# Cross-attention on one core: shared products issued whole at the end of a head, value bias on TensorE, residual and row normalisation off VectorE

## What is computed

```python
q = jnp.einsum('oc,bct->bot', Wq, target) + bq[None, :, None]
k = jnp.einsum('oc,bcs->bos', Wk, source) + bk[None, :, None]
v = jnp.einsum('oc,bcs->bos', Wv, source) + bv[None, :, None]
...
dot = jnp.einsum('bhdt,bhds->bhts', q, k) / math.sqrt(HEAD_DIM)
mask = target_mask[:, :, :, None] * source_mask[:, :, None, :]
dot = mask * dot - (1.0 - mask) * NEG
amap = jax.nn.softmax(dot, axis=-1) * mask
out = jnp.einsum('bhts,bhds->bhdt', amap, v)
```

## Time and profile before

| what | value |
|---|---|
| median of 3 runs | 3245.24 us (3241.58 to 3249.78) |
| profiled execution | 3250.03 us, span 3248.2 us |
| TensorE busy | 2971.8 us, 91% |
| VectorE busy | 2824.2 us, 87% |
| ScalarE busy | 2360.5 us, 73% |
| GpSimd busy | 1990.9 us, 61% |
| attention stage | about 1757 to 2836 us of the span |

### The profile page before, as it was taken

One profiled execution on the slowest core, in us unless ns is written; L12 is line 12 of the kernel. 1 busy time (PEld: TensorE's weight loads), 2 busy tenths in 40 slices (PEclk: granted clock), 3 DMA queues, 4 the chain that ended last, 5 costly groups with the idle time before them and its releaser, 6 DMA issues. The chain is left out here.

```text
span 3248.2 us, 47812 instructions
## 1 busy us (share of the span) xinstructions
PE 2971.8 (91%) x16101; PEld 1814.1 (56%) x16134; DVE 2824.2 (87%) x4149; ACT 2360.5 (73%) x4499; POOL 1990.9 (61%) x1071
## 2 busy tenths in 40 slices
PE   8899999999999999999976998888889888789998
PEld 5677777776777767776653433333333333244444
DVE  6999999999999999999995788888788888188886
ACT  5888888888888888888871366666666666567876
POOL 4999999999999999999993132232223222100000
PEclk9999999999999999999986699999999999899999
DMA  4202220122202220122224455555555553131111
GB/s 172 68 9 78 82 79 28 61 79 79 73 18 78 82 79 32 58 79 79 86 78 115 126 164 168 179 173 161 173 163 169 167 179 92 65 109 46 43 43 36
DMA packets 138148, 312.49 MB, mean 96 GB/s; under 512 B 20240, under 2 KB 27536, under 8 KB 137760
## 3 DMA queue, kind: packets, MB, share of 16 engines
q1 hardware_dynamic: 132544, 300.05, 29.3%
q10 hardware_dynamic: 5360, 9.38, 1.0%
HBM read 217.42 MB, written 91.95 MB: 95 GB/s over the span
## 5 line engine op out<-in xcount | busy, mean ns | idle before, releaser
L823 POOL TENSOR_TENSOR bu<-du,bc 128x1024 f32<-128x1024 f32 x512 | 1199.4, 2372 | 32.3 <-DMA bc<-bc_scratch 32.0
L710 ACT ACTIVATE states<-dt,negA 128x256 f32<-128x256 f32 x2048 | 852.6, 463 | 239.5 <-DVE hc L918 229.0
L1560 DVE TENSOR_REDUCE mmax<-s_ps 128x1 f32<-128x512 f32 x1024 | 671.7, 685 | 202.8 <-PE s_ps L1292 185.5
L906 DVE TENSOR_TENSOR_SCAN states<-states,bu 128x512 f32<-128x512 f32 x704 | 821.4, 1212 | 9.0 <-ACT states L710 8.1
L1416 ACT ACTIVATE pt<-s_ps 128x512 f32<-128x512 f32 x1024 | 549.0, 595 | 342.6 <-PE s_ps L1302 341.7
L918 DVE TENSOR_TENSOR hc<-states,bc 128x512 f32<-128x512 f32 x704 | 445.2, 673 | 1.2 <-DMA bc<-bc_scratch 1.2
L1292 PE MATMUL s_ps<-kst,qst 51*128 51x512 f32 x1024 | 400.0, 470 | 40.8 <-DMA kst<-mask_d 21.4
L528 PEld LDWEIGHTS y_ps<-id_sb,hc 128*128 128x128 f32 x2816 | 331.1, 143 | 122.4 <-DVE hc L918 58.0
L528 PE MATMUL y_ps<-id_sb,hc 128*128 128x128 f32 x2816 | 377.1, 277 | 23.4 <-DVE hc L918 23.4
L1302 PE MATMUL s_ps<-qst,kst 53*128 53x512 f32 x1024 | 385.5, 455 | 4.3 <-ACT pt L1416 4.3
L832 POOL TENSOR_TENSOR hp<-hp,bc 128x1024 f32<-128x1024 f32 x160 | 379.7, 2373 | 1.6 <-DVE hp L906 1.1
(11 more groups left out here) (164 smaller groups left out, 4218.8 us busy)
## 6 DMA issues: line engine op xcount, KB each, us to landing
bc<-bc_scratch SPq DMA_DIRECT2D x128, 512.0 KB, 5.0
stack_d<-parts SPq DMA_DIRECT2D x90, 512.0 KB, 3.8
qst<-stack_d SPq DMA_DIRECT2D x128, 192.0 KB
kst<-stack_d SPq DMA_DIRECT2D x128, 192.0 KB
x<-xres SPq DMA_DIRECT2D x31, 512.0 KB, 4.4
w_raw<-in_w_ffn SPq DMA_DIRECT2D x48, 256.0 KB, 2.7
w_raw<-in_w_ffn SPq DMA_DIRECT2D x16, 768.0 KB, 7.2
xT_sb<-in_xT SPq DMA_DIRECT2D x16, 512.0 KB, 5.9
```

The costliest lines, as they stand in the source:

```text
L710: a = act.activation(states[:, bank, first:first + SEQ], dt[:, t, :], ACT.Exp, scale=negA[:, t, c * NS + n:c * NS + n + 1])
L823: pool.tensor_tensor(bu[:, buf, :].rearrange("p (n l) -> p n l", n=NS), du[:, t % (2 * GRP):t % (2 * GRP) + 1, :].to_broadcast([P, NS, SEQ ...
L906: dve.tensor_tensor_scan(dst, src, bu[:, BU_OF[k][0], cols], 0.0, ALU.mult, ALU.add).then_inc(scan_done, 1)
L1560: dve.tensor_reduce(mmax[:, u // HG, c:c + 1], s1_ps[:, n % S_BANKS], AX.X, ALU.max).then_inc(s1_free, 1)
```

## The change

1. **TensorE.** A shared product is issued whole behind the fourth pair of its unit. The wait for `misc` moves there too. The value projections get the bias as two more fp32r products (128 by 256) from `pick` (ones in rows 0 and 32) and `bvs` (the bias's rounded part in row 0, its rest in row 32), so `vtmp` and VectorE's L1598 go.
2. **ScalarE.** `mask_values` reads `misc` itself, in unit u+1. `copy_back` copies the turned output from `misc` to `back_sb`. The maxima are copied in unit u+1 instead of u. These stand behind the first two exponentials, ahead of rounding and `copy_values`.
3. **GpSimd.** `add_back` adds `back_sb` to the residual (units 11 and 14), `normalise` (L1514 of the new kernel) and the scaling of the mask, `quarter_mask` (L1521), run in unit 0 behind the reciprocal root.
4. **VectorE.** It keeps the maxima, the statistics, k/q and the turns.

```diff
-                        if tt == 1 or tt == 3:
-                            shared_part(u, tt // 2)
+                    for pos, (unit, kind, _, off) in enumerate(MISC):
+                        if unit == u and has(kind, b + off):
+                            shared(pos, b, par)
...
                     for a in range(2):
                         st = 2 * idx + a
                         for k in range(SEQT):
+                            m = pe.matmul(misc[:, a * SEQ:(a + 1) * SEQ], ctx_sb[:, 1 - par, k, st * P:(st + 1) * P],
+                                          wv_sb[:, k, :], start=(k == 0), stop=False)
+                        m = pe.matmul(misc[:, a * SEQ:(a + 1) * SEQ], pick[:, :].bitcast(F32R), bvs[:, :].bitcast(F32R),
+                                      start=False, stop=True)
...
+            def copy_back(n, idx):
+                act.wait_ge(mm["back"], seq("back", n, idx))
+                if not (n == 0 and idx == 0):
+                    act.wait_ge(x2_added, n * 2 + idx)
+                act.activation(back_sb[:, :], misc[:, :], ACT.Copy).then_inc(ev["back"], 1)
...
+            def normalise(f):
+                if not (isinstance(f, int) and f == 1):
+                    pool.wait_ge(x1n_out, (f - 1) * 16)
+                for i in range(SEQT):
+                    m = pool.tensor_scalar(x1n[:, i, :], x1r[:, i, :], mv[:, i, 0:1], rs[:, i:i + 1], ALU.subtract, ALU.mult)
+                m.then_inc(ln_done, 1)
...
+            def add_back(n, idx):
+                if idx == 0:
+                    pool.wait_ge(xres_in, (n + 1) * 16)
+                pool.wait_ge(ev["back"], seq("back", n, idx))
+                pool.tensor_tensor(xres[:, idx, :], xres[:, idx, :], back_sb[:, :], ALU.add).then_inc(x2_added, 1)
...
-                    dve.tensor_tensor(vtmp[:, :, :], misc[:, :].rearrange("p (a o) -> p a o", a=2),
-                                      bv_sb[:, :].rearrange("p (a o) -> p a o", a=1).to_broadcast([P, 2, SEQ]),
-                                      ALU.add).then_inc(ev["v"], 1)
...
-                    dve.tensor_tensor(xres[:, idx, :], xres[:, idx, :], misc[:, :], ALU.add).then_inc(ev["back"], 1)
```

More of the change, by code:

```diff
@@ L1265, in body @@
                 if active(n):
[L1266 removed]
+                    wait(x2_added, n * 2 + 2)
                     sp.dma_start(rows(x2, n, SEQ * HID).rearrange("(i p h) -> p i h", p=P, h=HID), xres[:, :, :]).then_inc(x2_out, 16)
@@ L1316, in values, with shared @@
                     m.then_inc(pv_done, 1)
[L1318 removed]
+            def shared(pos, b, par):
                 _, kind, idx, off = MISC[pos]
                 batch = b + off
[L1322 to L1334 removed]
+                before = misc_before(pos, b)
+                if before is not None:
+                    pe.wait_ge(*freed(*before))
+                else:
+                    pe.wait_ge(kq_params, 3 * 16)
+                if isinstance(b, int) and b == -1 and kind in "mv":
+                    pe.wait_ge(params, 4 * 16)
+                    pe.wait_ge(vaug_set, 1)
                 if kind in "kq":
[L1337 removed]
+                    if kind == "k" and isinstance(batch, int) and batch == 1:
                         pe.wait_ge(ctx1_in, 16)
[L1339 removed]
+                    elif kind == "k":
                         pe.wait_ge(ctx_in, batch * 16)
[L1341 removed]
+                    if kind == "q":
                         pe.wait_ge(ln_done, batch)
@@ L1346, in shared @@
                             cols = slice(a * (HID // 2), (a + 1) * (HID // 2))
-                            product(misc[:, cols], w[:, k, idx * P:(idx + 1) * P], src[:, k, cols], k == 0, k == SEQT - 1)
+                            m = pe.matmul(misc[:, cols], w[:, k, idx * P:(idx + 1) * P], src[:, k, cols],
+                                          start=(k == 0), stop=(k == SEQT - 1))
                 elif kind == "v":
-                    if part == 0 and isinstance(batch, int) and batch == 0:
+                    if isinstance(batch, int) and batch == 0:
                         pe.wait_ge(ctx_in, 16)
+                        pe.wait_ge(bvs_ready, 1)
                     for a in range(2):
@@ L1371, in shared @@
                         m = pe.transpose(misc[0:HG * TT, i * P:(i + 1) * P], mmax[:, g, :], id2[:, :])
-                    m.then_inc(mm["m"], 1)
-                cuts = [0, len(products) // 2, len(products)]
-                for dst, lhsT, rhs, start, stop in products[cuts[part]:cuts[part + 1]]:
-                    if kind in ("turn", "back"):
-                        m = pe.transpose(dst, lhsT, rhs)
-                    else:
-                        m = pe.matmul(dst, lhsT, rhs, start=start, stop=stop)
-                if products and part == 1:
-                    m.then_inc(mm[kind], 1)
+                m.then_inc(mm[kind], 1)
             def body(b, par):
                 s, n = b + 1, b - 1
-                def shared_part(u, part):
-                    for pos, (unit, _, _, off) in enumerate(MISC):
-                        if unit == u and has(MISC[pos][1], b + off):
-                            shared(pos, b, par, part)
                 for u in range(HEADS):
@@ L1483, in body @@
                             mask_values(b + off, 1 - par, idx)
+                        if unit == u - 1 and kind == "back" and active(b + off):
+                            copy_back(b + off, idx)
+                    for kind, unit in SPLIT_AT.items():
+                        if u == unit and active(f):
+                            round_part(kind, f)
+                    if u % HG == HG - 1:
+                        g, batch = (u // HG - 1, b) if u >= HG else (HGROUPS - 1, n)
+                        if active(batch):
+                            copy_values(batch, g)
+                    if active(b):
+                        exponentials(b, u, 1)
                     if u == 14 and active(f + 1):
                         if active(b + 1):
-                            act.wait_ge(ev["v"], (b + 1) * 2 + 2)
+                            act.wait_ge(v_masked, (b + 1) * 2 + 2)
                         load_ctx(f + 1, 1 - par)
@@ L1620, in body @@
                     for unit, kind, idx, off in MISC:
-                        if unit == u - 1 and kind != "m" and has(kind, b + off):
+                        if unit == u - 1 and kind in ("k", "q", "turn") and has(kind, b + off):
                             evacuate(kind, b + off, idx, 1 - par if off % 2 else par)
```

105 lines of the change are left out of this document (42 added, 63 removed).

## The result

The changed kernel took 3154.99 us (median of 4 runs, 3150.34 to 3156.56) against 3245.5 for the kernel before (4 runs, 3241.58 to 3249.78): ratio 0.9718, 95% interval 0.9702 to 0.9735. The profiled execution took 3153.5 us, 96.5 less than that of before.

What follows compares the result with a forecast made beforehand. TensorE's work was put at 55.2 of 63.56 us a batch, the rest waits, mostly for `misc`. Gains of 4.0 a batch (52 over 13), plus 3, 1.4 and 2, less 1.6, made 57: 3188 us, range 3165 to 3222.

Steps and rivals of the forecast that it cites:

- The wait for `misc`: TensorE before shared products: most of 8.3 us of waits a batch; in units 2 to 4 it goes, 15.23 to 13.4.
- units 5 to 9: Four turns and maxima: VectorE is late next, so the stretch falls from 17.83 to 15.8 us.
- the statistics are exposed: Units 0 and 1: VectorE's 1.93 us of statistics still delay unit 1's fourth pair; units 14 to 1 take 13.9.
- half a k, q or v product 1.06: TensorE's work per unit: two such halves added to a plain unit's 2.34 us make 4.46 with k, q or v.
- the first batch: b = -1, at low clock: k products start 6.5 instead of 7.89 us apart; gain 3 us after the bias.
- the last stretch: Last root to feed-forward stage (b = 13, 14, 15, tail): a gain of 4.4 us.
- The tail: Residual there is serial, two copies of 0.6 and two GpSimd additions of 1.04: loses about 1.6 us.
- (a): Rival, everything hides: VectorE freer than counted, batches near TensorE's own work; 58 us a batch, 3167 us; chance 0.1.
- bare bound: Extreme of the everything-hides rival: a batch takes only TensorE's 55.9 us, total 3145 us.
- (b): Rival, bias 0.53 a product and `misc` freed 0.5 later at four uses: gain 2 a batch, 3216 us; chance 0.15.
- (c): Rival: maxima's trip through DRAM grows 8 us, past 2.5 slack, stopping unit 0's first pair; 3260 us; chance 0.05.
- (d): Rival, no change: waits only move, say to values waiting for exponentials behind copies; 3245 us; chance 0.05.

Runs made afterwards that it cites:

- moves alone: Changed kernel with the shared products again in halves behind the second and fourth pair: 3261.0 us, ratio to the kernel before 1.0041.
- halves late: Changed kernel with the shared products in halves behind the third and fourth pair: 3202.0 us, ratio to the kernel before 0.9861.
- the repetition above: Second run of the kernel before with only the shared products made whole behind the fourth pair: 3153.5 us, ratio 0.9710.
- the interleaved order: Changed kernel with early statistics, aggregates at unit 14 and turns spread to units 4, 6, 8, 10: 3141.1 us, ratio to the kernel before 0.9682.

## Why the prediction missed

**Right.** The wait for `misc` was the loss, and the place behind the fourth pair takes it away (50.6 us in the window, now 0.2); the idle before k and q is gone. VectorE bounds units 5 to 9 (15.73 for 15.8) and the statistics are exposed before unit 1's fourth pair (units 14 to 1: 13.91 for 13.9; 1.24 us come back when they are moved). v starts late by at most 0.17 (2210.03, with the pair before it at 2209.53). The moves cost and give little: normalisation 0.1 a batch, costed at nothing. GpSimd's new work hides.

**The step that failed: "half a k, q or v product 1.06", taken twice for a whole ("one with k, q or v 4.46").** The half was read from its start to the pair behind it and holds the cost of that edge; the unit takes 4.24. The whole takes 1.92, and a turn or back 0.59 (2244.17 to 2244.76) instead of 2 x 0.37. Where TensorE bounds, this is 0.2 x 3 of the 0.7 us in units 2 to 4. In units 10 to 13 it is 0.2 for each v and 0.15 for each back, 0.7 of the 1.1; the bias, 0.12 for 0.17, is 0.2 more, and the rest is that `misc` was free earlier than counted. Together 1.8 us a batch. The halves behind the third and fourth pair show the price directly: 0.4 us for each cut product in units 2 to 4, where nothing waits. That the edge costs is shown; what it is about the edge stays open.

**A term that was not there: the granted clock at the two ends of the stage.** In the first batch the prediction kept 0.52 and took 3 us; it was 0.70 and 14. This goes with the whole products: in that window the three kernels with cut products (before, moves alone, halves late) have 0.52, 0.50 and 0.58, and all eleven profiled executions with whole ones 0.65 to 0.75. In the last stretch the prediction gave 4.4 us and 15.4 came. By the first reciprocal of a turn in each iteration, 10.0 of these were won up to unit 5 of b = 15, all at a clock of 1.00, where 6 had been given to b = 13 and 14: that is the mis-sized product again. From there to the tail's first turn before took 41.0 us at a clock of 0.79 and the changed kernel 33.7 at 1.00: 7.3 us where nothing had been put. How much of it is the clock and how much the whole products of b = 15 was not separated. The tail gave back 1.9. In before the clock was down from 2800 us, 37 us ahead of the feed-forward stage:

```profile
2800.00:2820.00 20.00, 17.99 (x69) 5.07 (x71) 0.69 (x1) 10.15 (x20) 0.00 (x0) 0.59 0.25 73
```

and in the changed kernel up until 2720, 20 us ahead of it:

```profile
2700.00:2720.00 20.00, 17.29 (x96) 5.90 (x96) 0.74 (x2) 17.06 (x34) 9.36 (x4) 1.00 0.03 13
```

By the repetition above this part need not be a property of the change; the last stretch differed by 22 us between two executions of one kernel. Why the clock rises in the first batch of some kernels, and falls in the last of some executions, was not settled.

**The tail** was rightly sized at a small loss: 1.9 us for 1.6, by ScalarE's copy and GpSimd's addition, 0.60 and 1.26, twice in series.

**The rivals.** (a) gave the right batch, 58, for a reason that is wrong: VectorE is no freer than counted, and TensorE's own work is less. Its bare bound is added up wrongly: 55.9 us a batch gives 3141 with the same edges, not 3145; nothing rests on it. (b) fell on both counts, bias 0.12 and `misc` late by 0.17 at most. (c) did not happen in this change, but is the limit that the interleaved order meets 1.5 us a batch further on; its slack was overstated, 2.5 for 0.3: from the first issue to a pair that waited for it 4.76 us went by, where 3.3 were put, and the units ahead of it gave more than 2. (d) fell.

## What to carry to other kernels

The duration of a piece that lies between two of another kind holds the cost of its edges; before two pieces are added up to a whole, look for a row in which they lie together, or take the edges off. When several engines share one buffer by turns, move the product as far from the last consumer as the loop allows before moving work between the engines: here place and wholeness gave 6.0 us a batch in a two-line edit (with the moves in, 4.1 for the place and 2.6 for the wholeness), and all moves together cost 0.25. Stages at the start and the end, with less work for TensorE, need a bound of their own for the granted clock, in both directions.

## What was not expected of the hardware

- **An edge between full-row products and pairs costs.** Cutting four fp32 products of 128 rows in two, with a pair of 51 and 53 rows between, costs 0.20 us (2 x 1.06 against 1.92) and 0.1 in each pair; for transposes 0.15 (2 x 0.37 against 0.59). An fp32r product in the midst of fp32 ones cost only 0.12, so the number format alone is an unlikely reason.
- **A tiny VectorE instruction can wait for a long one of GpSimd.** An addition over 128x2, SBUF to SBUF, took 1.60 and 3.87 us instead of 0.17, each time until the conversion on GpSimd ended, while statistics and aggregates beside the same conversion kept their durations. Whether it costs anything depends on the place: nothing in unit 12 of one order, 5 us a batch in another.
- **GpSimd's one-input work has two prices.** 512 columns took 2.08 us with two scalars from SBUF and 0.62 with constants; the first is 0.54 on VectorE.
- **The granted clock can fall after one idle time.** The same idle time of 2.70 us on TensorE was followed by some 4 to 12 us of a lower clock in nine batches and by none in a tenth; with the idle gone, by moving one instruction of VectorE, every window of the batch was at 1.00.
- **The same program's last batch ran at 1.00 or at 0.50**, 164.7 or 186.9 us.

The fastest version found is the changed kernel with the statistics in units 11 and 12 of the iteration before: 3133.6 us, ratio to before 0.9635 (0.9605 to 0.9666), faster than both. Whole products and GpSimd normalisation without the other moves, together with early statistics, were not tried; an estimate by the measured parts is some 0.37 us a batch less.
